# Loop 1 of a two-layer graph and expert kernel: the sums that TensorE takes of |m| and of the edge products once per eight blocks

## The reference, cut to what matters

```python
# stage 1 (graph layer 0), on layernorm(x)
adj0 = A * (y @ y.T)
row_l1 = max(sum(abs(adj0), axis=1), 1e-12)
x = x + 0.9 * (adj0 / row_l1) @ layernorm(x) + 0.1 * h0
# stage 2: shared feed-forward (gelu) plus the top 2 of 8 experts, hidden size 512
# stage 3 (graph layer 1), on layernorm(x), needs one number per node of adj alone:
edge_i = sum_j adj[i, j] * adj[j, i]
# stage 4: top 2 of 8 experts, hidden size 256
```

## Time and profile before

| | |
|---|---|
| median of three runs | 1471.12 us |
| profiled execution: its own time | the page prints none beside the span |
| profiled execution: span, first to last instruction | 1555.4 us |
| PE busy | 1367.5 us, 88% of the span |
| DVE busy | 929.2 us, 60% |
| ACT busy | 649.6 us, 42% |
| POOL busy | 461.5 us, 30% |
| loop 1, first L726 to last L742 | 12.9 to about 714 us of the span |

### The profile page before, as it was taken

One profiled execution on the slowest core, in us unless ns is written; L12 is line 12 of the kernel. 1 busy time (PEld: TensorE's weight loads), 2 busy tenths in 40 slices (PEclk: granted clock), 3 DMA queues, 4 the chain that ended last, 5 costly groups with the idle time before them and its releaser, 6 DMA issues.

```text
span 1555.4 us, 21717 instructions
## 1 busy us (share of the span) xinstructions
PE 1367.5 (88%) x6536; PEld 829.7 (53%) x6536; DVE 929.2 (60%) x2670; ACT 649.6 (42%) x1108; POOL 461.5 (30%) x450
## 2 busy tenths in 40 slices
PE   5998999999999999998689999999999998766771
PEld 2443444444444444456578877466666666545550
DVE  6775858576776767684322224777777777432224
ACT  3454344343444433444244344565555555422220
POOL 2102021111202020213545554223323332465652
PEclk9999999999999999999899999999999999978885
DMA  9688988696888787875366442889888888433435
GB/s 314 253 335 315 337 297 305 239 341 238 321 274 317 265 318 266 304 248 206 104 250 223 170 165 96 312 296 311 296 292 308 304 287 250 117 111 113 126 109 202
DMA packets 117360, 386.22 MB, mean 248 GB/s; under 512 B 20116, under 2 KB 49587, under 8 KB 87824
## 3 DMA queue, kind: packets, MB, share of 16 engines
q1 hardware_dynamic: 77296, 327.32, 60.9%
q10 hardware_dynamic: 27136, 33.93, 6.2%
q0 software_dynamic: 12832, 23.81, 4.3%
HBM read 332.80 MB, written 57.41 MB: 251 GB/s over the span
## 4 chain that ended last, share of the span: by engine, by line
PE 51%; issue 12%; DVE 10%; another core or an unknown queue 5%; ACT 4%; POOL 3%; DMA 2%; DVEq 0%; POOLq 0%; ACTq 0%; SPq 0%
PE agg L742 14%; PE d L846 7%; PE s L726 6%; PE d L790 4%; POOL rows_scratch L1798 3%; PE d L800 2%; PE d L680 2%; DVE adj_over_wb L386 2%; PE agg L913 2%; PE u L831 2%; PE u L833 2%; ACT h L1101 2%; PE u L827 1%; PE u L832 1%
## 5 line engine op out<-in xcount | busy, mean ns | idle before, releaser
L742 PE MATMUL agg<-m,xn 128*128 128x512 f32 (+1 forms) x800 | 399.4, 585 | 0.0
L1065 ACT ACTIVATE mabs<-m 128x512 f32<-128x512 f32 (+1 forms) x400 | 243.7, 619 | 322.4 <-DVE m L1561 289.4
L1561 DVE TENSOR_TENSOR m<-s,ring 128x512 f32<-128x512 f32 (+1 forms) x400 | 268.2, 676 | 184.2 <-PE s L726 127.7
L726 PE MATMUL s<-ymov,ysta 128*128 128x512 f32 (+1 forms) x400 | 244.8, 616 | 42.7 <-DVE m L1561 24.7
L1798 POOL DMA_INDIRECT rows_scratch<-xrow,idx x160 | 183.8, 1149 | 297.8 <-DVE xrow L1306 102.8
L1807 POOL DMA_INDIRECT y_scratch<-yo,ids x164 | 160.9, 981 | 138.9 <-DVE yo L1456 70.8
L742 PEld LDWEIGHTS agg<-m,xn 128*128 128x128 f32 x800 | 152.2, 191 | 62.8 <-issue 41.9
L726 PEld LDWEIGHTS s<-ymov,ysta 128*128 128x128 f32 x400 | 75.3, 190 | 199.7 <-issue 97.8
L386 DVE TENSOR_TENSOR adj_over_wb<-ring,adj_over_wb 128x512 fp32r<-128x512 f32 (+1 forms) x216 | 138.8, 672 | 48.5 <-ACT adj_over_wb L1165 44.7
L1784 POOL TENSOR_TENSOR rstd<-vareps,mhalf 128x4 f32<-128x4 f32 x30 | 38.3, 1277 | 405.6 <-DVE vareps L1218 405.6
L1165 ACT CAST adj_over_wb<-ring 128x512 fp32r<-128x512 f32 (+1 forms) x216 | 125.6, 607 | 45.7 <-PE agg L920 42.6
(11 more groups left out here) (242 smaller groups left out, 1982.8 us busy)
## 6 DMA issues: line engine op xcount, KB each, us to landing
ring<-in_adj_in SPq DMA_DIRECT2D x180, 1024.0 KB
ring<-in_adj_out SPq DMA_DIRECT2D x30, 1024.0 KB
wb<-blob_scratch SPq DMA_DIRECT2D x27, 834.0 KB
rows_scratch<-yo ACTq DMA_DIRECT2D x81, 260.0 KB, 6.7
stage<-in_adj_out SPq DMA_DIRECT2D x19, 1024.0 KB
ring<-in_adj_in SPq DMA_DIRECT2D x20, 784.0 KB
xt<-rows_scratch SPq DMA_DIRECT2D x54, 260.0 KB
wbz<-blob_scratch SPq DMA_DIRECT2D x27, 193.0 KB
```

The lines of the kernel that those rows point to most:

```text
L726: pe.matmul(sbank[s % 2][:, 0:n], ysta[:, s * P:(s + 1) * P], ymov[:, k % 2, 0:n], start=True, stop=True).then_inc(s_made, 1)
L742: pe.matmul(abank[:, 0:n], xn[:, b, :], m[:, b % M_BUFS, 0:n], start=b == 0, stop=b == NB - 1).then_inc(S["agg_blocks"], 1)
L1065: act.activation(mabs[:, b % ABS_BUFS, 0:width(k)], m[:, b % M_BUFS, 0:width(k)], ACT.Abs).then_inc(abs_made, 1)
L1561: dve.tensor_tensor(m[:, s % M_BUFS, 0:width(k)], sbank[s % 2][:, 0:width(k)], slot_part(LOAD_AT[k, l, False][0], s % LB, width(k)), ALU.m ...
```

## The change

PE does the sums in steps 10, 18, 26, 34 and 42 alone, each time for the two groups that are complete: first both sets of |m|, then both sets of edge products. At step 42 the |m| sums of group 9 come last, behind the edge products, as before. Nothing else is touched: no other engine's code, no buffer, no order of loads.

```diff
-                if agg and s >= 6 and s % GROUPS == 2:
-                    l = s // GROUPS - 1
-                    if l < LOADS - 1:
-                        add_abs(k, l)
-                    if l in PAIRS[k] and l != k:
-                        add_cols(k, l)
-                    if l == LOADS - 1:
-                        add_abs(k, l)
+                if agg and s >= 2 * GROUPS and s % (2 * GROUPS) == 2:
+                    both = (s // GROUPS - 2, s // GROUPS - 1)
+                    for l in both:
+                        if l < LOADS - 1:
+                            add_abs(k, l)
+                    for l in both:
+                        if l in PAIRS[k] and l != k:
+                            add_cols(k, l)
+                    if both[1] == LOADS - 1:
+                        add_abs(k, LOADS - 1)
```

## The result

The changed kernel takes 1479.7 us, the median of six runs (1476.72 to 1482.36); the kernel before took 1470.95 in six runs beside them (1469.55 to 1473.01). The ratio is 1.0058, with a 95% interval of 1.0045 to 1.0071: **by the ratio 8.5 us slower, between 6.6 and 10.4**. Forecast were 1469.8 us and a range of 1462 to 1479; rival B had 1477.7 and rival C 1479.8.

What follows compares the result with a forecast made beforehand. PE was taken to bound loop 1 nearly everywhere except chunk 2. The terms -9.2 - 0.8 + 1.2 + 11.5 - 4.0 gave -1.3 us from 1471.12, so 1469.8 us, range 1462 to 1479.

Steps and rivals of the forecast that it cites:

- rival B: Slower by chunk 2: SP's queue between steps 6 and 10, 22 and 26 costs 13 us, holds stay; 1477.7 us, chance 0.27.
- rival C: Merged visits save nothing, as the 0.33 us belongs to each set's start; +8.7 us, 1479.8 us, chance 0.03.
- term 4: Chunks 3 and 4: DVE's holds during POOL's row scatter get covered by the sums of step 34; -4.0 us.
- term 3: Chunk 2: outgoing pieces of loads 2 and 6 come late, as PE's sums free their slots later; +11.5 us.
- term 1: Fewer visits to the 32-column sums: 0.33 us saved in each of 28 windows outside chunks 0 and 2; -9.2 us.
- term 2: 12 windows outside chunk 2 with two loads of edge products, where DVE falls behind PE: +0.1 each, +1.2 us.
- Chunk 0: Waits for inputs in places, so half of its five saved visits was counted: -0.8 us, bounds -1.65 and 0.
- second stall: Chunk 2, load 6's piece behind load 4's: wanted in step 25, sums now in step 26 instead of 22; +5.6 us.
- mark-up of 2.8 us: Slow clock after PE's idle time at chunk 2's two stalls, about 1.4 us more each; left out of the sum.
- ACT's new wait: ACT's \|m\| of a window's first block waits for PE's sums, about 2 us later; costed at nothing.

Runs made afterwards that it cites:

- second profile: The kernel before the change, unedited, profiled once more because its first profile was stretched by 84 us: 1472.68 us, ratio 0.9995.
- experiment 8: Changed kernel, but single visits in all of chunk 2 and in the windows where double ones had not saved: 1461.64 us, ratio 0.9933 to the kernel before.
- experiment 7: Changed kernel, but SP issues nothing behind load 2's late outgoing piece in chunk 2 until it has landed: 1479.22 us, ratio 1.0042 to the kernel before.
- experiments 6 and 7: The first: changed kernel with incoming pieces of loads 3 and 7 ahead of outgoing pieces of loads 2 and 6 in chunk 2, 1480.47 us; the other: see experiment 7.

## Why the prediction was wrong

Two steps failed: term 4 took -4.0 us from a hold of DVE that isn't there in the second profile, and term 3, right in its mechanism, was mis-sized at +11.5 where chunk 2 measured +16.2. Measured terms are those of the window table, second profile of before.

- **Terms 1 and 2, the visits: the price of a visit right, both terms off, their sum near by luck.** The 0.33 us a visit that the earlier trace rows gave is 0.30 to 0.37 in 29 of the 40 windows outside chunks 0 and 2, so rival C falls: a merged visit does save it. That rival C's time of 1479.8 is the nearest of all is chance. But the 28 windows of term 1 gave -6.6 and not -9.2: five of them lost, among them the third windows of chunks 1, 5 and 9, where "PE bounds" did not hold. The 12 windows of term 2 gave -2.1 and not +1.2: nine saved their 0.3 or more, and three lost 0.35 to 0.51 (the third of chunks 3 and 4, the second of chunk 9), where DVE's extra work stands close together (experiment 8). In sum -8.0 was forecast and -8.7 measured.
- **Chunk 0: -0.8 forecast, about +0.8 measured.** The table's +3.05 is one profile against one. The seven profiles with double visits in all of chunk 0 have 65.4 to 67.6 us for it, mean 66.4; the three with single ones throughout 64.9 to 66.0, mean 65.6. The first window alone scatters by 2.4 us whatever the visits, so the sign of the whole is not sure. The third window is: 12.51 to 12.52 us in all seven with a double visit, 11.64 to 11.66 in all seven with single ones.
- **Term 3, chunk 2: the mechanism right, both places right, the size too small.** +11.5 forecast, bounds 7 and 16, measured +16.2. Its own working doesn't quite give 11.5: the stalls are 6.0 + 5.6 = 11.6, and five saved visits at 0.33 would leave 10.0. The second stall was forecast at 5.6 and its window measured 6.6. The first was forecast at 6.0 and the first two windows measured 9.3 (1.36 + 7.94). By the working's own dates, counted from the chunk's first `s`, the piece should have been used at 27.1 us and was used at 32.5, 5.3 later. Of this, 3.2 are issue to use: I took 4.8 to 5.0 us, as for a piece that has the transfers to itself, and it took 8.0; experiment 7 shows 1.5 of it to come from the three issues behind it, and puts the rest beside ACT's writes. 1.7 are the start of step 10, at 20.0 us into the chunk and not at 18.2 as in the first profile. The rest is the visit, which began 0.3 us later into the step than taken.
- **The slow clock ahead of step 10: not in the sum, and worth about 1.1 us there.** Of the 1.7 us, 0.6 are that step 6 began later: DVE waited 5.35 us for `blob_scratch<-wlow` where it had waited 4.74 in the first profile, which no term of mine touched. The rest lies between the `s` of step 6 and that of step 10. Changed kernel, then experiment 7, with the same visits:

```profile
154.47:162.81 8.34, 7.76 (x17) 3.82 (x17) 8.02 (x22) 2.50 (x4) 0.00 (x0) 0.59 0.11 41
...
152.03:159.22 7.19, 5.96 (x18) 2.52 (x16) 7.12 (x20) 2.50 (x4) 0.00 (x0) 1.00 0.13 47
```

At a granted clock of 1.00 these four steps take 7.19 us, and 7.19 too in the first profile of before with a visit among them (152.63 to 159.82, clock 1.00), so DVE did set the pace, as I wrote. In the changed kernel, behind a stand of PE of 3.21 us, the clock was 0.59, between the levels 1.2 and 2.4 GHz, and they took 8.34. It is no effect of the change alone: in the second profile of before PE stood still ahead of step 6 too, for some 3.7 us, the clock was 0.79, the four steps took 8.20 and step 10 began at 20.4 us. Against that profile step 10 was not late. The Trainium skill, page "TensorE: Matmul & The Clock Gate", Part 1, says that idle time puts the array back to 1.2 GHz; the trace agrees in the direction. The mark-up of 2.8 us that I worked out from it and left out was for the time behind the stalls; it would have brought the sum nearer, but what can be read off is the price ahead of the first.
- **Term 4, the held DVE: wrong, -4 forecast, nothing measured.** It was read from one execution that was stretched by 84 us, and what the earlier trace rows show isn't in the second profile: against the first profile the fourth windows of chunks 3 and 4 are 4.6 and 4.5 us shorter, against the second 0.3 each, one visit. I had written that I couldn't place those 84 us, and still took a term from a stand that nothing explained. The Trainium skill, page "SBUF — State Buffer", section "SBUF: two separate sides", has the port pair that VectorE and GpSimd share locked for one instruction at a time; by it the term was 0, as measured.
- **The sum** with measured terms is -8.7 + 0.8 + 16.2 + 0 = +8.3 us, where the runs gave +8.5; that it fits to 0.2 is partly chance, since chunk 2's term comes from one pair of profiles. Of the 9.6 us between this sum and the forecast's -1.3, 4.7 are term 3, 4.0 term 4 and 1.6 chunk 0; terms 1 and 2 take 0.7 back. Rival B named this end and its place, and had 0.27; its own price of 13 us was too low too.

PE in chunk 2 of the changed kernel, around step 10 (start, us; two `s` of the same shape at either clock, then the double visit):

```profile
161.33 1.18 PE L726 MATMUL s<-ymov,ysta 128*128 128x512 f32 x1
...
162.81 0.80 PE L726 MATMUL s<-ymov,ysta 128*128 128x512 f32 x1
...
164.39 1.92 PE L792 MATMUL d<-mabs,picks 128*32 128x512 f32 x16
166.13 1.90 PE L802 MATMUL d<-ring,picks 128*32 128x512 f32 x16
```

The visit itself was as forecast: 1.74 us for two sets of |m|, and load 0's edge sums done one set later. ACT's new wait is there, for PE's |m| sums (L792), and costs nothing that shows: windows with it save their 0.33 us all the same, and DVE waited for ACT's |m| 6.3 us in all of loop 1, against 5.4 in the second profile of before. The waits of the changed kernel's loop 1:

```profile
ACT mabs L1067 <- PE d L792: 134.1, 35, 4.8
...
DVE m L1563 <- ACT mabs L1067: 6.3, 7, 2.6
```

## What to carry to other kernels

Before batching small visits of an engine, ask what each of them frees: one that frees a buffer with a waiting transfer behind it is on the transfer's path, and its delay is paid about one for one, while the others can be merged. When the profiled execution is longer than the timed ones by more than the effect in question, take no term from a stall that nothing explains; profile again first. A transfer that starts late also meets other traffic than it did before. And batch only where the engine that does the visits is the bound: where the other one has extra work in the stretch, here the router's instructions beside edge products, the short visits had given it time to catch up.

## What the runs showed of the hardware

- Two profiled executions of one kernel differed by 88.6 us in their span (1555.4 and 1466.8), 20 of them in loop 1 and 68 behind 1300 us, while all timed runs of that kernel lay between 1467 and 1493.
- A transfer of 1 MB from SP took 5.0 us from issue to use with one issue close behind it, 4.7 with two within 0.9 us, 6.5 with none behind it but 1.04 MB of ACT's writes beside it, and 8.0 with both, those writes and two or three issues of SP within 3 us (experiments 6 and 7).
- Four steps of the loop took 7.19 us at a granted clock of 1.00 and 8.34 at 0.59, with the same PE instructions in both (the `s` of step 6 to that of step 10, chunk 2, changed kernel and experiment 7).
- After 8.4 us of waiting in the changed kernel's chunk 2, PE's granted clock was 0.62 over the next 6 us, and the first pair of `agg` took 1.91 us instead of 1.02:

```profile
178.39 0.80 PE L726 MATMUL s<-ymov,ysta 128*128 128x512 f32 x1 [8.37 <-DVE m L1563]
178.99 1.91 PE L742 MATMUL agg<-m,xn 128*128 128x512 f32 x2
```
